# One buffer instead of two for the memory operands, and three steps moved by a slot, in a fused decoder layer

## The reference, cut to what matters

```
q, k   = split(x @ w_attn.T + b_attn)           # 16 heads of 32 channels, v = x
y_ar   = softmax(causal(q k^T * scale)) v
k2     = x[:, :-1] @ w_k2.T + b_k2
qa     = -leaky_relu(-q[1:] * scale, 0.02)
ka     = sigmoid(k2 * scale * 0.02)             # computed as 0.5 * (tanh(z / 2) + 1)
y_ma   = causal(qa ka^T) (v[1:] - y_ar[:-1])    # no softmax
out    = (y_ar + y_ma) @ w_proj.T + 2 * b_proj
```

## Time and profile before

| | us |
|---|---|
| median of three executions | 1741.72 |
| profiled execution, its own time | 1741.72 |
| its span, first to last instruction | 1740.0 |
| TensorE busy | 1666.7 (96%) |
| VectorE busy | 1263.1 (73%) |
| GpSimd busy | 1164.5 (67%) |
| ScalarE busy | 979.7 (56%) |
| TensorE's share of the chain that ended last | 77% |

### The profile page before, as it was taken

One profiled execution on the slowest core, in us unless ns is written; L12 is line 12 of the kernel. 1 busy time (PEld: TensorE's weight loads), 2 busy tenths in 40 slices (PEclk: granted clock), 3 DMA queues, 4 the chain that ended last, 5 costly groups with the idle time before them and its releaser, 6 DMA issues.

```text
span 1740.0 us, 30895 instructions
## 1 busy us (share of the span) xinstructions
PE 1666.7 (96%) x10626; PEld 1110.6 (64%) x10626; DVE 1263.1 (73%) x2785; ACT 979.7 (56%) x1939; POOL 1164.5 (67%) x965
## 2 busy tenths in 40 slices
PE   6999999999999889999998999999999999999998
PEld 5677677676776458877853556565565656656566
DVE  5677777778777667777866767868777686777745
ACT  4565665666655443333355666666566666666654
POOL 2556565665655555654477878878698787879774
PEclk9999999999999899999999999999999999999999
DMA  7566565655655454667445534425443453533210
GB/s 205 149 163 171 156 170 151 172 157 156 179 137 159 148 182 151 193 190 217 150 136 133 151 89 118 118 69 151 104 122 98 103 139 83 152 97 99 63 42 31
DMA packets 167272, 237.29 MB, mean 136 GB/s; under 512 B 22086, under 2 KB 73286, under 8 KB 167116
## 3 DMA queue, kind: packets, MB, share of 16 engines
q1 hardware_dynamic: 167116, 235.31, 48.9%
HBM read 91.57 MB, written 41.94 MB: 77 GB/s over the span
## 4 chain that ended last, share of the span: by engine, by line
PE 77%; POOL 7%; DVE 4%; DMA 4%; issue 4%; ACT 3%; SPq 2%; POOLq 0%; ACTq 0%; DVEq 0%
PE bank L1655 9%; PE bank L201 7%; PE bank L202 7%; PE bank L203 7%; POOL cross_added L1977 6%; PE bank L1525 5%; PE bank L1493 5%; PE bank L305 5%; PE bank L1464 5%; PE bank L369 4%; PE bank L356 4%; PE bank L327 2%; PE bank L1561 2%; PE bank L1539 2%; PE bank L903 1%
## 5 line engine op out<-in xcount | busy, mean ns | idle before, releaser
L1474 DVE TENSOR_REDUCE cross_negmax<-bank 128x1 f32<-128x512 f32 x512 | 339.0, 675 | 149.3 <-PE bank L1464 146.8
L1741 ACT ACTIVATE cpt<-bank 128x512 f32<-128x512 f32 x512 | 297.8, 596 | 142.6 <-PE bank L1493 139.1
L430 ACT ACTIVATE pt<-bank 128x256 f32<-128x256 f32 (+3 forms) x512 | 219.8, 439 | 231.7 <-PE bank L305 228.3
L554 DVE CUSTOM_DVE_ANT_0 bank<-bank,future 128x128 f32<-128x128 f32 (+3 forms) x512 | 243.1, 493 | 115.2 <-PE bank L356 111.0
L1977 POOL TENSOR_TENSOR cross_added<-cross_added,cpt 128x2048 f32<-128x2048 f32 x61 | 279.9, 4589 | 11.3 <-ACT cpt L1741 10.9
L1493 PE MATMUL bank<-cqk 98*128 98x512 f32 x512 | 226.0, 441 | 7.5 <-ACT cpt L1741 7.2
L619 POOL TENSOR_SCALAR_AFFINE_SELECT pt<-pt 128x512 f32<-128x512 f32 x128 | 81.5, 637 | 223.6 <-ACT pt L430 223.6
L1464 PE MATMUL bank<-cqk 96*128 96x512 f32 x512 | 212.4, 418 | 11.1 <-DVE cross_negmax L1474 8.9
L1977 POOL TENSOR_TENSOR cross_added<-cpt,cpt 128x2048 f32<-128x2048 f32 x32 | 146.7, 4583 | 83.1 <-ACT cpt L1741 83.1
L305 PE MATMUL bank<-qk 98*128 98x256 f32 (+2 forms) x512 | 181.3, 357 | 8.6 <-ACT pt L430 4.3
L201 PE MATMUL bank<-xt_hi,w_hi 128*128 128x512 f32 x384 | 157.1, 409 | 16.2 <-DVE w_lo L506 13.2
(11 more groups left out here) (207 smaller groups left out, 3605.0 us busy)
## 6 DMA issues: line engine op xcount, KB each, us to landing
qk<-stage SPq DMA_DIRECT2D x384, 128.0 KB, 2.4
cqk<-cstage SPq DMA_DIRECT2D x384, 128.0 KB, 2.3
scratch_memory<-memory SPq DMA_DIRECT2D x32, 512.0 KB, 3.8
ma<-scratch_memory SPq DMA_DIRECT2D x32, 512.0 KB, 4.0
raw<-in_x_t SPq DMA_DIRECT2D x32, 256.0 KB, 3.1
v<-in_x SPq DMA_DIRECT2D x32, 256.0 KB, 3.3
scratch_y_ar<-y_ar SPq DMA_DIRECT2D x32, 256.0 KB, 2.6
my_ar<-scratch_y_ar SPq DMA_DIRECT2D x32, 256.0 KB, 4.5
```

Source lines behind the costliest of these rows:

```text
L554: dve.tensor_tensor_reduce(out=scores, in0=scores, in1=sh.future[:, SEQ - P * (qt + 1):SEQ], scale=-1.0, scalar=-NEG, op0=ALU.add, op1=ALU ...
L1474: dve.reduce_max(s.negmax[gm % 2][:, col:col + 1], max_bank(sh, m)[:, :], AX, negate=True).then_inc(s.dve_max, 1)
L1741: act.activation(s.pt[step % 3][:, j, :], sh.bank[2 + n % 2][:, :], ACT.Exp, scale=SCALE_CROSS).then_inc(s.act_exp, 1)
```

## The change

The second memory tile is gone, and with it 4096 bytes of each partition that nothing else takes; the tiles laid out behind it in this phase move down. All writes of the tile now wait for the store of the group before. Three steps move: the third step of the K2 projection from slot 1.0 to 0.3, ahead of the sums; the plus one from slot 2.2 to 2.0; and the low half of K behind the maximum of its slot. SP no longer waits for the store before.

```diff
-        self.memory, self.relu = [sb(f"memory{i}", [P, 2, SEQ]) for i in range(2)], sb("relu", [P, SEQ])
+        self.memory, self.relu = sb("memory", [P, 2, SEQ]), sb("relu", [P, SEQ])
...
-PROJECTED = {(0, 0): (2, 7), (0, 1): (2, 8), (0, 2): (2, 9), (1, 0): (2, 10), (1, 1): (2, 11), (2, 0): (3, 0),
+PROJECTED = {(0, 0): (2, 7), (0, 1): (2, 8), (0, 2): (2, 9), (0, 3): (2, 10), (1, 1): (2, 11), (2, 0): (3, 0),
...
-            if d >= 2:
-                act.wait_ge(s.memory_stored, 16 * (d - 1))
+            if d >= 1:
+                act.wait_ge(s.memory_stored, 16 * d)
...
-        if kt == 2 and j == 2 and 0 <= g + 2 < NG:
+        if kt == 2 and j == 0 and 0 <= g + 2 < NG:
             d = g + 2
-            ka = s.memory[d % 2][:, 1, 1:SEQ]
+            ka = s.memory[:, 1, 1:SEQ]
...
-        if kt == 0 and j == 2 and 0 <= g + 2 < NG:
-            d = g + 2
-            st = s.stage[d % 2]
-            dve.wait_ge(s.act_k, d + 1)
-            dve.scalar_tensor_tensor(out=st[:, 3, :].bitcast(F32R), in0=sh.bank[6][:, :], scalar=bias_column(s, K, d),
-                                     in1=st[:, 2, :], op0=ALU.add, op1=ALU.subtract).then_inc(s.dve_k, 1)
         m = n + SELF_LEAD
...
+        if kt == 0 and j == 2 and 0 <= g + 2 < NG:
+            d = g + 2
+            st = s.stage[d % 2]
+            dve.wait_ge(s.act_k, d + 1)
+            dve.scalar_tensor_tensor(out=st[:, 3, :].bitcast(F32R), in0=sh.bank[6][:, :], scalar=bias_column(s, K, d),
+                                     in1=st[:, 2, :], op0=ALU.add, op1=ALU.subtract).then_inc(s.dve_k, 1)
...
-            if d >= 2:
-                dve.wait_ge(s.memory_stored, 16 * (d - 1))
+            if d >= 1:
+                dve.wait_ge(s.memory_stored, 16 * d)
...
-                sp.wait_ge(s.pool_ones, 5)
-            else:
-                sp.wait_ge(s.memory_stored, 16 * d)
+                sp.wait_ge(s.pool_ones, 4)
```

More of the change, by code:

```diff
@@ L572, in self_vector @@
                                      in1=st[:, 0, :], op0=ALU.add, op1=ALU.subtract).then_inc(s.dve_q, 1)
-            if d >= 2:
-                dve.wait_ge(s.memory_stored, 16 * (d - 1))
-            dve.scalar_tensor_tensor(out=s.memory[d % 2][:, 0, :], in0=sh.bank[7][:, :], scalar=bias_column(s, Q, d),
+            if d >= 1:
+                dve.wait_ge(s.memory_stored, 16 * d)
+            dve.scalar_tensor_tensor(out=s.memory[:, 0, :], in0=sh.bank[7][:, :], scalar=bias_column(s, Q, d),
                                      in1=s.relu[:, :], op0=ALU.add, op1=ALU.subtract).then_inc(s.dve_q, 1)
@@ L604, in self_gpsimd @@
     ones_rows(pool, s.kq, s.pool_ones)
-    for memory in s.memory:
-        pool.memset(memory[:, 1, 0:1], 0.0).then_inc(s.pool_ones, 1)
+    pool.memset(s.memory[:, 1, 0:1], 0.0).then_inc(s.pool_ones, 1)
     for g in range(-3, 0):
@@ L680, in self_sync @@
             if d == 0:
-                sp.wait_ge(s.pool_ones, 5)
-            else:
-                sp.wait_ge(s.memory_stored, 16 * d)
-            sp.dma_start(t["memory"][d // GROUPS, d % GROUPS][:, 0:2, :], s.memory[d % 2][:, :, :]).then_inc(s.memory_stored, 16)
+                sp.wait_ge(s.pool_ones, 4)
+            sp.dma_start(t["memory"][d // GROUPS, d % GROUPS][:, 0:2, :], s.memory[:, :, :]).then_inc(s.memory_stored, 16)
         if kt == 3 and j == 0 and 0 <= g + 1 < NG:
```

## The result

The changed kernel took 1753.45 us (median of five) against 1744.24 us for the kernel before (also the median of five, the three named before the prediction among them). The ratio is 1.0058, 95% interval 1.0045 to 1.0073: slower by 10 us. The forecast was 1747.6 us and a range up to 1753.0; the direction was right, the size too small. The profiled execution after took 1750.89 us, with a span of 1749.2 us against 1740.0 us, so the two traces differ by 9.2 us.

The account below looks back on a forecast made before the run. The prediction took TensorE, busy 91.67 of 92 us at full clock in mid-phase, as the bound. It added 3.5 (steady), 1.3 (start) and 1.1 (middle and end), 5.9 us, to 1741.72, giving 1747.6 us, range 1740.5 to 1753.

Parts of the forecast that it names:

- 0.12 us a group: Steady cost of moving the K2 step to slot 0.3, in groups 1 to 29: 3.5 us in all.
- Its part for the tanh: ScalarE's chain starts later, so the tanh and the Q step of slot 2.0 come 0.09 us later a group.
- a tie: VectorE's maximum of slot 1.3 ends about when L356 of slot 2.2 needs its bank: 0.03 us a group, 0.13 with restart.
- The sign that the prediction named for its own cause: In the changed profile, L201's wait for the tanh would be larger, 0.35 us a group, and more frequent.
- The upper bound of my range for this term: Steady cost of the K2 step with the full restart cost: 0.22 us a group, +6.4 us.
- The start: Later stack loads make TensorE wait 0.78 us longer for group 1's stack and 0.51 for group 2's: 1.3 us together.
- The middle and the end: Later loads cost 0.6 us over four slow-load groups and 0.5 at the late wait for rows of maxima: 1.1 us.
- The low half of K: In the usual group, its place behind the maximum holds nothing, as TensorE's sums now start at 302.71: 0.
- One tile: The store lands 1.2 us before L575 of the next group needs the tile, so the single tile costs 0.
- Rival B: The single tile binds: late store landings in a third of the groups add 8 us, about 1755 us; chance 0.10.
- Rival A: The shift is absorbed: steady term -1 to +1 us, start 1.3, middle nothing or 1, about 1743 us; chance 0.30.
- Rival C: Faster: the step in slot 0.3 hides TensorE's gaps around the sums, 0.21 us a group, 1736.9 us; chance 0.10.

Follow-up runs that it names:

- e2: Kernel before with only the low half of K moved behind the maximum of slot 0.2: ratio 1.0068, spacing 18.32 us a group.
- e5: Changed kernel with the low half of K back in front of the maximum of slot 0.2: ratio 1.0034 against the kernel before.
- e3: Kernel before with one memory tile and its waits, no step moved: ratio 1.0005, spacing 18.00 us.
- e10: Changed kernel with SP issuing the rows of maxima ahead of the memory store: ratio 1.0049 against the kernel before, spacing 18.22 us.
- e4: Changed kernel with the last of a group's four reciprocals moved from slot 1.2 to 1.3, behind that slot's maximum: ratio 1.0068, spacing 18.15 us.
- e7: Kernel before with the tanh ahead of slot 1.2's exponential and the first Q step ahead of slot 2.0's L305: ratio 0.9966, spacing 17.68 us.
- e8: e7 with SP issuing the rows of maxima ahead of the memory store: ratio 0.9921 against the kernel before, 1729.05 us.

## Why the prediction was right or wrong

**Its steps in the group.** The moves of the sums, the exponentials, the tanh and the maxima came out within 0.06 us of the forecast, on ScalarE and on VectorE. The step that failed is the term "0.12 us a group", 3.5 us in the sum: it measured 0.23 us a group, 6.7 us in 29 groups. Its part for the tanh, 0.09, measured 0.05. It was mis-sized at L356 of slot 2.2, which I called a tie and gave 0.03 us, with 0.13 as the other end. It is a wait in 25 of 26 groups. The instruction is 0.10 us later than the 309.16 at which it would stand with the tanh's part, and the projection step follows it by 0.29 us instead of 0.19. The sign that the prediction named for its own cause did not come either: L201's wait for the tanh was to grow to 0.35 us and come more often, and it fell, from 20 times to 18 (4.3 us instead of 5.3). The upper bound of my range for this term, 0.22, was the right value, and it alone would have given 1750.5 us. The prediction reached it with 0.09 for the tanh and 0.13 for the tie, where 0.05 and 0.18 were measured, so the match is in part luck.

**The start.** 1.3 us were forecast and 3.0 measured. The mechanism (loads late by the new order, and TensorE's wait for head 0 of group 1 longer) was right, e2 and e5 show it. The second wait came as forecast: 0.5 us longer for the stack of group 2 (0.77 us in the changed kernel against 0.27). The first was to be 0.8 us longer and was 2.5. The sum took the median landing of 2.4 us for each transfer, though the earlier trace rows had one of 10.9 us on record; the third transfer of head 0 took 4.1. So two things were missing: the gap in the transfers, which the delay moved onto head 0, and the clock. The clock fell within the wait of 3.7 us and stayed at the lower level until 46.8 us, 5.6 us behind the wait's end, and in that time the rows of maxima came late.

**The middle and the end.** 1.1 us forecast. The 29 groups cost 0.2 us beyond the spacing (6.86 less 29 x 0.23) instead of 0.6, the end 0.9 instead of 0.5: L305 waited 3.04 us for the rows of maxima there instead of 2.13. That the sum comes to 1.1 is luck.

**The low half of K** in mid-phase: 0 forecast, 0 in the change, but only because the K2 step stands there; alone it is 0.32 us a group (e2). The forecast said that TensorE's sums were not held since they start at 302.71; that was right.

**One tile**: 0 forecast, and e3 and e10 agree. Rival B is out. Rival A, 0.30, had the start right in kind but not the steady part. Rival C would have needed the tanh ahead of 306.4; it stood at 306.55. Nor did the step hide the gap ahead of the sums: they start 0.33 us after the matmul before them (308.84 to 309.17), 0.1 more than one matmul after another.

**The sum.** By the profiled executions: 3.0 + 6.9 + 0.9 - 1.5 = 9.2 us with rounding, against 5.9 forecast. The time itself is off by 5.9 us, 1753.45 against 1747.6. Of these, 3.3 are the terms above: the term per group is 3.2 us short and the start 1.7, and the 1.5 us of the rest of the program go the other way. The other 2.5 are the median of the kernel before, which more runs put at 1744.24 instead of 1741.72.

## What to carry to other kernels

When an instruction of the bounding engine is moved ahead of a hand-off, follow the hand-off on each engine behind it until the next time the bounding engine waits for that engine; where the forecast ends in a tie, work out what losing it costs, restart included, and give that end its weight; here it was lost in nearly every group. An edit that is free in the steady state is still to be followed through the start and the end, where the loads have no room, and a wait of some microseconds there can cost the clock as well. Small transfers that the bounding engine waits for are worth trying ahead of large ones that nobody waits for; here that order gained little with 18.00 us a group and more with 17.68. And where an edit removes one wait on a chain, look for the next deadline on the same chain first, as e4 did not.

## What the runs showed of the hardware

In this kernel a short wait of TensorE costs some 0.1 us more than its length. Behind the wait of 0.25 us in the earlier trace rows, the second matmul starts 0.33 us after the first, and the third 0.24 after the second:

```profile
307.26 0.50 PE L201 MATMUL bank<-xt_hi,w_hi 128*128 128x512 f32 x1
307.59 0.40 PE L202 MATMUL bank<-xt_hi,w_lo 128*128 128x512 f32 x1
307.83 0.39 PE L203 MATMUL bank<-xt_lo,w_hi 128*128 128x512 f32 x1
```

In the changed kernel L356 of slot 2.2, after its wait, is followed after 0.29 us (315.69 to 315.98), where 0.19 stood before.

The transfers have gaps of about 1 us in which at most two of the 16 DMA engines are busy although transfers are under way. From 30 to 600 us each of the two traces has eight of 0.8 to 1.3 us, and each begins 0.6 to 1.8 us after the start of a 16 KB packet of an instruction queue; but there are 27 such packets, and most are followed by a shorter gap or none. Whether the packet is the cause was not tested. At the start the gap moved by 0.4 us between the two kernels while the loads moved by 1.05.

What is issued right behind the 512 KB store on the same queue lands later than ahead of it: the two rows took 3.6 us as the median in e7 and 2.5 in e8. The Trainium skill ("DMA: Bandwidth & Descriptors", Queues, rings and completion order) says that a completion is written only after all earlier writes of that DMA engine; e8 fits this, with the two transfers of 8 KB each on time as soon as they stand ahead of the store, but it does not tell this cause from mere queueing.
